# Layer norm sums over the feature blocks: eight fp32 matmuls each, against one strided VectorE reduction and one matmul

## The reference

```python
def _layernorm(x, axis=-1, eps=1e-5):
    m = jnp.mean(x, axis=axis, keepdims=True)
    v = jnp.var(x, axis=axis, keepdims=True)
    return (x - m) / jnp.sqrt(v + eps)

# ffn: y = real(ifft(fft(x) @ (w_real + i*w_imag))) + bias
# attn: q = x @ Wq, k = v = x (16 heads of 64), scores = tril(q k^T), out = scores v
x = x + 0.5 * ffn(layernorm(x))
x = x + attn(layernorm(x))
x = x + 0.5 * ffn(layernorm(x))
```

## Time and profile before

| | us |
|---|---|
| median of 3 runs | 3234.86 |
| lowest, highest of the runs | 3234.35, 3370.32 |
| the profiled execution | 3235.95 |
| its span on the slowest core (core 5) | 3234.4 |
| spans of the 8 cores | 3211.1 to 3234.4 |
| share of the span: TensorE, VectorE, ScalarE busy | 73%, 24%, 10% |

### The profile page before, as it was taken

One profiled execution on the slowest core, in us unless ns is written; L12 is line 12 of the kernel. 1 busy time (PEld: TensorE's weight loads), 2 busy tenths in 40 slices (PEclk: granted clock), 3 DMA queues, 4 the chain that ended last, 5 costly groups with the idle time before them and its releaser, 6 DMA issues.

```text
span 3234.4 us, 30174 instructions; the slowest of 8 cores (3211.1 to 3234.4 us)
## 1 busy us (share of the span) xinstructions
PE 2362.9 (73%) x12032; PEld 1172.1 (36%) x12032; DVE 773.4 (24%) x756; ACT 320.0 (10%) x441; POOL 34.3 (1%) x68
## 2 busy tenths in 40 slices
PE   0788889947777777778757875787578757866785
PEld 0333334413353335234423542353236323622362
DVE  1100000013231323231323132313232322232223
ACT  1000000011010111010111011101110111101010
POOL 0000000000000000000000000000000000000000
PEclk9999999978888878888888887888788878887888
DMA  6000000020001000100010001000100010001000
GB/s 208 0 0 1 1 1 1 1 80 1 0 1 52 1 1 1 52 0 1 1 52 1 1 1 52 1 1 1 52 0 1 1 52 1 1 13 40 1 1 26
DMA packets 23860, 56.59 MB, mean 17 GB/s; under 512 B 4016, under 2 KB 4272, under 8 KB 23728
## 3 DMA queue, kind: packets, MB, share of 16 engines
q1 hardware_dynamic: 18608, 37.89, 3.9%
q0 software_dynamic: 5120, 16.78, 1.5%
HBM read 37.88 MB, written 16.78 MB: 17 GB/s over the span
## 4 chain that ended last, share of the span: by engine, by line
PE 70%; DVE 10%; issue 8%; ACT 5%; DMA 4%; SPq 2%; DVEq 0%; ACTq 0%; POOL 0%; POOLq 0%
PE ps_att L479 13%; PE ps_rot L479 9%; PE ps_att L211 8%; PE ps_rot L398 6%; PE ps_att L406 5%; PE ps_rot L211 5%; PE ps_scr L544 4%; PE ps_att L474 4%; DVE bufB L433 3%; PE ps_att L465 3%; PE ps_rot L474 3%; DMA bufA<-xT 3%; PE ps_scr L211 3%; ACT bufH L436 2%; PE ps_att L595 2%
## 5 line engine op out<-in xcount | busy, mean ns | idle before, releaser
L398 PE MATMUL ps_rot<-bufA,s_ones 128*128 128x512 f32 x256 | 138.1, 689 | 185.5 <-DMA bufA<-xT 169.1
L406 PE MATMUL ps_att<-bufG,s_ones 128*128 128x512 f32 x384 | 174.4, 597 | 3.6
L465 PE MATMUL ps_rot<-bufH,sMh 128*128 128x512 bf16 x192 | 62.7, 459 | 152.5 <-ACT bufH L436 152.5
L544 PE MATMUL ps_scr<-bufE,bufB 64*128 64x128 f32 x1024 | 158.4, 315 | 19.8 <-ACT bufF L528 12.8
L544 PEld LDWEIGHTS ps_scr<-bufE,bufB 64*128 64x128 f32 x1024 | 144.9, 222 | 33.7 <-issue 33.7
L474 PE MATMUL ps_rot<-bufH,sMh 128*128 128x512 bf16 x192 | 62.6, 458 | 122.3 <-DVE bufI L440 117.5
L479 PE MATMUL ps_att<-bufI,sMh 128*128 128x512 bf16 x640 | 151.2, 379 | 0.0
L479 PE MATMUL ps_att<-bufH,sMl 128*128 128x512 bf16 x640 | 151.2, 379 | 0.0
L398 PEld LDWEIGHTS ps_rot<-bufA,s_ones 128*128 128x128 f32 x256 | 53.8, 221 | 262.4 <-issue 262.4
L440 DVE SCALAR_TENSOR_TENSOR bufI<-bufB,bufH 128x2048 bf16<-128x2048 f32 x48 | 110.0, 2293 | 111.3 <-ACT bufH L436 93.0
L489 DVE SCALAR_TENSOR_TENSOR ftmp<-ps_att,isrep 128x512 f32<-128x512 f32 x80 | 55.3, 692 | 307.0 <-PE ps_att L479 307.0
(11 more groups left out here) (155 smaller groups left out, 2757.6 us busy)
## 6 DMA issues: line engine op xcount, KB each, us to landing
bufA<-xT SPq DMA_DIRECT2D x64, 256.0 KB, 8.4
outT<-bufC POOLq DMA_DIRECT2D x64, 256.0 KB, 8.6
sWtmp<-wrt SPq DMA_DIRECT2D x8, 512.0 KB, 15.9
sWtmp<-wit SPq DMA_DIRECT2D x8, 512.0 KB, 9.9
sCh<-cosh SPq DMA_DIRECT2D x8, 256.0 KB, 5.7
sCl<-cosl SPq DMA_DIRECT2D x8, 256.0 KB, 7.7
sNh<-sinh SPq DMA_DIRECT2D x8, 256.0 KB, 9.2
sNl<-sinl SPq DMA_DIRECT2D x8, 256.0 KB, 10.6
```

What stands on the lines that cost most here:

```text
L398: last = e.matmul(ps_rot[:, 0:512], s_ones[:, :], fb(zF, i), start=(i == 0), stop=(i == NFB - 1))
L406: last = e.matmul(ps_att[:, 0:512], s_ones[:, :], fb(bufG, i), start=(i == 0), stop=(i == NFB - 1))
L465: last = e.matmul(slot, wh[:, 1024 * kb + 128 * db:1024 * kb + 128 * (db + 1)], fb(bufH, kb), start=(kb == 0), stop=False)
L544: return e.matmul(ps_scr[0:128, 128 * h:128 * h + 128], kv, q, start=(h % 4 == 0), stop=(h % 4 == 3), tile_position=(64 * half, 0))
```

## The change

In `layer_norm` each sum of eight matmuls gives way to one VectorE `tensor_reduce` that adds up the eight blocks token by token (128x4096 in, 128x512 out, through a view in which the block is the innermost axis), and one matmul with ones on its result. Two buffers of 128x512 fp32 hold the results. Lines below the new buffers stand 1 or 2 lines further down in the changed kernel. The steps behind, mean and variance and so on, are as they were.

```diff
+        sqt0 = E0(nc.sbuf_tensor("sqt0", [128, 512], F32))
+        sqt1 = E0(nc.sbuf_tensor("sqt1", [128, 512], F32))
...
-            for h_ in range(2):
-                def s1(e, h_=h_):
-                    for i in range(4 * h_, 4 * h_ + 4):
-                        last = e.matmul(ps_rot[:, 0:512], s_ones[:, :], fb(zF, i),
-                                        start=(i == 0), stop=(i == NFB - 1))
-                    return last
-                cstep(PE, s1, reads=[zn + ":" + "ab"[h_], "s_ones"], writes=["psR"])
-
-            for h_ in range(2):
-                def s2(e, h_=h_):
-                    for i in range(4 * h_, 4 * h_ + 4):
-                        last = e.matmul(ps_att[:, 0:512], s_ones[:, :], fb(bufG, i),
-                                        start=(i == 0), stop=(i == NFB - 1))
-                    return last
-                cstep(PE, s2, reads=["bufG:" + "ab"[h_], "s_ones"], writes=["psA0"])
+            z4 = zF[:, :].rearrange("p (f t) -> p t f", t=CH)
+            g4 = bufG[:, :].rearrange("p (f t) -> p t f", t=CH)
+            cstep(VE, lambda e: e.tensor_reduce(
+                sqt0[:, :].unsqueeze(2), z4, axis=mybir.AxisListType.X, op=ALU.add),
+                reads=[zn + ":a", zn + ":b"], writes=["sqt0"])
+            cstep(PE, lambda e: e.matmul(ps_rot[:, 0:512], s_ones[:, :], sqt0[:, :],
+                                         start=True, stop=True),
+                  reads=["sqt0", "s_ones"], writes=["psR"])
+            cstep(VE, lambda e: e.tensor_reduce(
+                sqt1[:, :].unsqueeze(2), g4, axis=mybir.AxisListType.X, op=ALU.add),
+                reads=["bufG:a", "bufG:b"], writes=["sqt1"])
+            cstep(PE, lambda e: e.matmul(ps_att[:, 0:512], s_ones[:, :], sqt1[:, :],
+                                         start=True, stop=True),
+                  reads=["sqt1", "s_ones"], writes=["psA0"])
```

More of the change, by code:

```diff
@@ L317, in build_program @@
         steady_names = ["swqh", "swql", "sbias", "smask", "sid", "sS", "murep", "isrep",
-                        "ftmp0", "ftmp1",
+                        "ftmp0", "ftmp1", "sqt0", "sqt1",
                         "bufA:a", "bufA:b", "bufB:a", "bufB:b", "bufC:a", "bufC:b",
```

## The result

The changed kernel's time stands to that of the kernel before as 1.0141, with a 95% interval of 1.0125 to 1.0157: 1.4% slower. (The ratio leaves out the executions in which the cores of a die ran at a lower clock and took longer.) The profiled execution took 3271.9 us against 3235.95 us. The forecast was 3148 us.

The account below looks back on a forecast made before the run. TensorE's summing matmuls were taken to bound each layer norm; two 4.43 us reductions plus 2.5 us give 11.4 us (middle 11.6), saving 11.0 us a chunk, 88 in all, from 3236 to 3148 us. Range: 3120 to 3365.

Parts of the forecast that it names:

- What bounds the kernel: Layer norm, input to variance: TensorE's 16 matmuls are the path, VectorE stands by; 17.6, 12.8 and 15.0 us before the change.
- The reduction's time: Each VectorE reduction of 4096 elements: 0.17 us fixed plus 1.04 ns an element, 4.43 us, twice on each layer norm's path.
- the gain of 88 us: Input to variance, three layer norms: 6.2, 1.2 and 3.6 us saved, 11.0 a chunk, 88 us in eight chunks.
- The line 3148 + 48 x (r - 4.43): Whole kernel's time in us for a reduction time r of 4.43 us or more; it crosses 3236 at r = 6.26.
- 2.5 us behind the second reduction: From second reduction to variance: gaps and one low-clock matmul, 2.5 us; mean and its square (1.7 us) hide behind that matmul.
- The clock at nothing: TensorE's longer idle around a layer norm costs nothing, as the dense stage already starts at low clock; otherwise 12 us.
- the first one: Rival in the reductions: the strided read takes a second cycle, 8.7 us each, kernel 3353 us; chance 0.39 including anything dearer.
- the middle case: Rival in the reductions: the stride costs half a cycle or so, 6.56 us each, kernel 3250 us; chance 0.15.
- The rule of the Trainium skill: SBUF reads: lines of 16 bytes, two hits on a line needed for full bandwidth, each new line pays; no VectorE price given.
- the two forms of a cost: Stride cost in the reductions: a second cycle or more (0.39, 3353 us), or half a cycle or so (0.15, 3250 us).
- the case without it: Reductions run at the contiguous rate, the stride costing nothing: 4.43 us each, kernel 3148 us; chance 0.44.
- both large cases: Whole kernel's time: contiguous rate at 3148 us (0.44) and a second cycle or more at 3353 us (0.39), either side of 3236.

Follow-up runs that it names:

- e2: Changed kernel with each reduction replaced by three contiguous VectorE additions, same mean and variance; ratio 0.9746 to the kernel before, profiled 3152.5 us.
- e3: Changed kernel with the input's sum back on TensorE's matmuls, only the squares' sum through the strided reduction; ratio 0.9869 to the kernel before, profiled 3189.3 us.
- e5: Against the kernel before: input's sum stays on TensorE, squares' sum goes through three contiguous VectorE additions and one matmul; ratio 0.9668, profiled 3124.6 us.
- e6: As e5, but the squares are added in halves, the first addition running while ScalarE squares the second half; ratio 0.9599 to the kernel before, profiled 3101.3 us.
- e7: Changed kernel with the squares' sum back on TensorE's matmuls, only the input's sum through the strided reduction; profiled 3297.9 us, no ratio on record.
- e1: Changed kernel with both reductions reading their 4096 elements in memory order, so sums are of the wrong elements; profiled 3150.1 us.

## Why the prediction was wrong, step by step

- *What bounds the kernel; the path from the input to the variance.* Right. By the table above 37 us of loss are expected from the intervals alone, and 36 were measured in the profiled execution, closer than the spread between cores allows one to count on. The same sum gives the time of the other kernels: 35.0 us in e2 is 8 x 10.4 = 83 us under 3236, so 3153 (3152.5 measured); 38.9 in e3 gives 3184 (3189.3); 31.4 in e5 gives 3124 (3124.6); 29.0 in e6 3105 (3101.3). Only e7 is further off, by 14 us.
- *The reduction's time: "I take 4.43, by L433, the row nearest in size, type and memory."* This is the step that failed. It measured 7.04 to 7.15 us, 7.09 in the mean, 1.7 ns an element. L433 was near in everything but the one thing that I had named as different, the step between neighbours. e1 shows that the rate itself was right (4.42 for contiguous reads) and that nothing but the step was missing. The term was mis-sized by 2.66 us, 48 times over: 128 us, which turns the gain of 88 us into a loss of 40 (36 in the profiled execution).
- *The line 3148 + 48 x (r - 4.43).* Right: with r = 7.09 it gives 3276, and 3272 were measured.
- *2.5 us behind the second reduction, mean and square hidden, squares in time.* Right: 16.62 - 7.15 - 7.05 = 2.4 us, and L417 waits for PE L408.
- *The clock at nothing.* Right, by the stretches behind the variance (24.7 to 25.4 us against 25.0 to 25.9), and by everything outside the intervals (2071 us against 2072).
- *The rivals.* The mechanism of the first one held, its price did not: not a second 1.04 ns on every element (8.7 us) but some six tenths of it, (7.09 - 4.43) / 4.27. So the time came out in the middle case, "half a cycle or so", to which I gave 0.15 and 3250 us. The rule of the Trainium skill that spoke for a cost was the right one to weigh; I gave the two forms of a cost 0.54 together and still named the case without it, because each form alone was less likely. That 3272 us lies between 3120 and 3365 is no credit to the sum: the range had been drawn to hold both large cases. L433's row could not speak against the first rival: it reads neighbours, as does every VectorE row of the kernel before.

## What to carry to other kernels

Before a sum over the outer axis of a buffer becomes one strided VectorE operation, count how many values it reads in a row from the same 16 bytes: with one fp32 value the reduction of 4096 took 7.1 us, while three contiguous additions took 4.2 for the same work. When work is moved from a busy engine to an idle one, keep both at work: with both sums on VectorE the two stand in a row, with one on each engine even the slow reduction was a gain (0.987), and the contiguous form gave 0.967, or 0.960 in halves. Look at what stands behind a waiting step in an engine's queue: one half of the change, with nothing behind the wait, was worth 47 us of gain, the other half, with eight matmuls behind it, 62 us of loss. (That turning the queue round would mend the second is an argument, not a run.)

## What the runs showed of the hardware that I had not expected

- The price of a strided fp32 read is nothing up to a step of 8 bytes, paid in part at 12 and in full from 16 on, where it hardly depends on the step: 4.42 us at 4 and 8 bytes, 5.56 (4080 values) at 12, then 7.40, 7.47, 7.03, 7.04 at 16, 32, 256 and 2048. Pairs of neighbours bring it back to 4.42.
- One strided operand costs nearly what two do: 3.68 us and 3.81 against 2.29 for a tensor_tensor of 2048. A strided write costs as much, 3.67.
- A tensor_scalar of 2048 goes from 1.23 to 2.05 us, a ScalarE copy from 1.91 to 3.77: ScalarE loses most.
- A reduction has no cost for closing a sum: 512 sums of eight and 64 sums of 64 take the same 4.42 us.
